# VectorE's mixing-table work in another order: differences in the second unit of four, carry scans in the last

## The chip, the cores and the metric

The kernel runs on one core of a Trainium2 chip. The metric is the device time of one execution in microseconds; the time before is 500.8 us, the median of three runs.

## The reference

Input x is 2 x 2048 tokens of 256 channels, float32. Cut to what matters:

```python
xn = layernorm(x)
# token mixing
k, v = xn @ key_w.T, xn @ value_w.T            # k is not used
r = sigmoid(xn @ recep_w.T)
aa, bb, pp = 0, 0, -10000
for t in range(T):                              # per batch row and channel
    ww = time_first + pp;  p = max(pp, ww)
    e1, e2 = exp(pp - p), exp(ww - p)
    wkv[t] = (e1*aa + e2*v[t]) / (e1*bb + e2 + 1e-6)
    ww2 = time_decay + pp; p2 = max(pp, ww2)
    e1b, e2b = exp(pp - p2), exp(ww2 - p2)
    aa = e1b*aa + e2b*v[t];  bb = e1b*bb + e2b;  pp = p2
attn = (r * wkv) @ out_w.T
# feed-forward: 8 experts, 2 for each token, and a shared one
gate = softmax(xn @ gate_w.T + gate_b); top 2 of 8
y = sum over the chosen e of gate_e * ((silu(xn@w1_e.T+b1_e) * (xn@w3_e.T+b3_e)) @ w2_e.T + b2_e)
z = (silu(xn@ws1.T+bs1) * (xn@ws3.T+bs3)) @ ws2.T + bs2
out = x + attn + y + z
```

The exponent pp, the decays e1b, the factors e1 and e2 and the sum bb depend on the time step and the channel only, not on x. So they can be computed once for all batch rows: 3 tables of 256 channels x 2048 steps. These are the mixing tables.

## The kernel before, in words

The program has three stages, written by hand for each engine, with semaphores between the engines and nothing that reorders: an engine runs its instructions in the order of the code.

1. `route`: the layer norm, the gate and the sorting of the tokens by expert.
2. `run_experts`: 71 tiles of 128 tokens go through their experts' weights, in 36 **units** `a` (`DUOS`): the first has one tile, the others two. Each product is made of three fp32r matmuls of high and low parts.
3. `mix`: eight steps of the token mixing, the shared expert and the sum.

The change lies in `run_experts`. What each engine does in unit `a` there:

- TensorE: turns the hidden rows (`turn_h(a)`, L1105, tile `ps_h`), turns the gathered tokens of unit a+3 (`turn_x`, L1079, `ps_x`), the down product of unit a-1 and the up product of unit a+2 (L1085, `ps_y` and `ps_g`). `turn_h(a)` waits for `hid` of unit a and for `h_lo` of unit a-1.
- ScalarE: silu of unit a+1 (L1161, `act`), the high parts of `ps_h` and `ps_x` (L1168, L1153), the result of unit a-1 (L1174), and pieces of the table work.
- VectorE: `hidden(a+1)` (L1249, tile `hid`, waits for that silu), `cut_h(a)` (L1256, `h_lo`), `cut_x(a+3)` (L1240, `x_lo`), and then its share of the table work.
- GpSimd: the indirect DMAs that gather the tokens of unit a+6 (L1008, `xg`), and its share of the table work. The gather of unit b waits until `turn_x(b-4)` is done (four buffers).
- SyncE: stores and loads.

The mixing tables are made beside this, in 8 **pieces** v of 256 time steps, four units for each. With v, r = divmod(a, 4), the work of piece v goes through these steps:

- `grown(v)`, VectorE: a copy of the last column to the first (L1264, `s_p`), then two scans (L1266) that give the exponent pp along the piece.
- `differences(v)`, VectorE: four scalar_tensor_tensor of 128x256 (L1277), (s_p + first) - s_p and (s_p + decay) - s_p, into `dif`, which lies in the tile `raw_vr` and has one buffer. It waits for `t_sides`, ScalarE's reading of the piece before.
- `halves(v)` and `exps(v)`, ScalarE: the positive and negative parts (L1182 to L1184, then `t_sides`) in unit 4v, and the exponentials (L1189 to L1194, with two loads of activation tables) in unit 4v+1. Piece 0 has both in unit 2.
- `scan_b(v)`, VectorE: a copy and two scans (L1286, L1289, `s_b`) in unit 4v+2; piece 0 has the scans alone in unit 3.
- `denominator(v)`, GpSimd: L1019, L1020 and L1022, tile `den`, in unit 4v+3 after the gather; it waits for `t_bb` (scan_b).
- `invert(v, 0..3)`, VectorE: four reciprocals of 128x128 (L1298), two in unit 4v+4, and one each in the next two.
- `factors(v)`, GpSimd: a product of 128x1024 (L1027) in unit 4v+6, once `t_rec` says that the fourth reciprocal is done.

In unit 24 GpSimd also makes the low parts of a table of biases (`low_rows`, L1033, L1034, L1037).

Before, `grown(v+1)` stood in unit 4v+1, ahead of the third reciprocal of piece v-1, and `differences(v+1)` in unit 4v+3. So VectorE's table work of a piece is: two reciprocals in r = 0; a copy, two scans and a reciprocal in r = 1; a copy, two scans and a reciprocal in r = 2; four differences in r = 3.

Of the kernel before, what the change touches and what calls it, by code (L numbers as in the profile page):

```python
# [85 lines left out]
def at_least(eng, sem, value):  # L86

    if isinstance(value, int) and value <= 0:
        return
    eng.wait_ge(sem, value)  # L90
# [766 lines left out]
def run_experts(nc, kept, placed, xn_d, y_d, y, y_stored, firsts1, coef_stored, tab_d, vec_tf, vec_td, ident, tile_tok, tile_exp,  # L857
# [3 lines left out]
    with ExitStack() as ctx:  # L861
# [6 lines left out]
        def sem(name):  # L868
            return kept.enter_context(nc.semaphore(name))
# [64 lines left out]
        t_dif = sem("t_dif")  # L934
# [18 lines left out]
        LAST_V = NPIECE - 1  # L953
# [279 lines left out]
        def vector(dve):  # L1233
            def cut_x(a):
                if a >= DUOS:
                    return
                n = tiles(a)
                dve.wait_ge(c_xhi, a + 1)
                at_least(dve, c_g, a - 1)
                nc.vector.tensor_tensor(x_lo[a % 2][:, 0:n], ps_x[:, 0:n], x_hi[a % 2][:, 0:n].bitcast(F32),  # L1240
                                        ALU.subtract).then_inc(c_xlo, 1)

            def hidden(a):
                if a >= DUOS:
                    return
                n = tiles(a)
                dve.wait_ge(c_silu, a + 1)
                at_least(dve, c_th, a)
                nc.vector.tensor_tensor(hid[:, 0:n, :], ps_g[a % 2][:, 0:n, FF:2 * FF], act1[:, 0:n, :],  # L1249
                                        ALU.mult).then_inc(c_h, 1)  # L1250

            def cut_h(a):
                n = tiles(a)
                dve.wait_ge(c_hhi, a + 1)
                at_least(dve, c_y, a - 1)
                nc.vector.tensor_tensor(h_lo[a % 2][:, 0:n], ps_h[:, 0:n], h_hi[a % 2][:, 0:n].bitcast(F32),  # L1256
                                               ALU.subtract).then_inc(c_hlo, 1)

            def grown(v):
                own = OwnIn(dve, t_own, At(0, v, NPIECE), 2)  # L1260
                if v == 0:
                    own.n += 1
                else:
                    own.link(nc.vector.tensor_copy(s_p[:, :, 0:1], s_p[:, :, PIECE:PIECE + 1]))  # L1264
                for c in range(KC):
                    ins = nc.vector.tensor_tensor_scan(out=s_p[:, c, 1:PIECE + 1],  # L1266
                                                       data0=grow[:, c:c + 1].broadcast_to([P, PIECE]),
                                                       data1=zero[:].broadcast_to([P, PIECE]),
                                                       initial=s_p[:, c, 0:1], op0=ALU.add, op1=ALU.add)
                own.link(ins)  # L1270
                own.close()

            def differences(v):
                at_least(dve, t_sides, v)
                for n, vec in enumerate((vec_tf, vec_td)):
                    for c in range(KC):
                        ins = nc.vector.scalar_tensor_tensor(out=dif[:, n, c, :], in0=s_p[:, c, 0:PIECE],  # L1277
                                                             scalar=vec[:, c:c + 1], in1=s_p[:, c, 0:PIECE],
                                                             op0=ALU.add, op1=ALU.subtract)
                ins.then_inc(t_dif, 1)  # L1280

            def scan_b(v):
                dve.wait_ge(t_exp, v + 1)
                if v > 0:
                    dve.wait_ge(t_den, v)
                    nc.vector.tensor_copy(s_b[:, :, 0:1], s_b[:, :, PIECE:PIECE + 1]).then_inc(t_carry, 1)  # L1286
                    dve.wait_ge(t_carry, v + 1)
                for c in range(KC):
                    ins = nc.vector.tensor_tensor_scan(out=s_b[:, c, 1:PIECE + 1], data0=decay[:, c, :],  # L1289
                                                       data1=one[:].broadcast_to([P, PIECE]), initial=s_b[:, c, 0:1],  # L1290
                                                       op0=ALU.mult, op1=ALU.add)
                ins.then_inc(t_bb, 1)

            def invert(v, i):
                c, h = divmod(i, 2)
                part = den[:, c, h * (PIECE // 2):(h + 1) * (PIECE // 2)]
                dve.wait_ge(t_den, v + 1)
                ins = nc.vector.reciprocal(part, part)  # L1298
                if i == 2 * KC - 1:
                    ins.then_inc(t_rec, 1)  # L1300

            def low_mask():
                own = Own(dve, c_mask)
                dve.wait_ge(c_iota, 1)
                own.link(nc.vector.tensor_scalar(row32[:], row32[:], TERMS - 1, None, ALU.bitwise_and))
                nc.vector.tensor_scalar(is_lo[:, 0:1], row32[:], float(3 * E + 1), None, ALU.is_equal)
                own.link(nc.vector.tensor_scalar(is_lo[:, 1:2], row32[:], float(2 * E), None, ALU.is_ge))
                own.link(nc.vector.tensor_tensor(is_lo[:, 1:2], is_lo[:, 1:2], is_lo[:, 0:1], ALU.subtract))
                own.mark(nc.vector.tensor_scalar(is_lo[:, 2:3], is_lo[:, 1:2], -2.0, 1.0, ALU.mult, ALU.add))
# [24 lines left out]
            for a in range(DUOS):  # L1334
                v, r = divmod(a, 4)
                hidden(a + 1)
                if a == DUOS - 1:
                    dve.wait_ge(c_whi, 2)
                    nc.vector.tensor_tensor(col[2][:], col[0][:], col[1][:].bitcast(F32), ALU.subtract
                                            ).then_inc(c_wlo, 1)  # L1340
                cut_h(a)
                cut_x(a + 3)
                if a < 2:
                    for i in range(12 + 2 * a, 14 + 2 * a):
                        split_lo(dve, i)
                if a == 1:
                    grown(0)
                    differences(0)
                if a == 2:
                    dve.wait_ge(t_dif, 1)  # L1350
                    grown(1)
                if a == 3:
                    scan_b(0)
                if r == 0 and 0 < v <= NPIECE:
                    invert(v - 1, 0)
                    invert(v - 1, 1)
                if r == 1:
                    if 0 < v < LAST_V:
                        grown(v + 1)
                    if 0 < v <= NPIECE:  # L1360
                        invert(v - 1, 2)
                    if v == NPIECE:
                        invert(v - 1, 3)
                if r == 2:
                    if 0 < v < NPIECE:
                        scan_b(v)
                    if 0 < v < NPIECE:
                        invert(v - 1, 3)
                if r == 3 and v < LAST_V:
                    differences(v + 1)  # L1370
                if a == A_ZERO + 2:
                    low_mask()

        return sync, gpsimd, tensor, scalar, vector, (c_y, c_yc, c_wlo, c_gT, c_rowsb)


# [483 lines left out]
```

## Time and profile before

| | |
|---|---|
| median of the runs | 500.8 us |
| the three runs | 498.76, 500.80, 504.41 us |
| span of the profiled execution, first to last instruction | 476.0 us |
| TensorE busy | 442.4 us (93%) |
| VectorE busy | 370.7 us (78%) |
| ScalarE busy | 241.5 us (51%) |
| GpSimd busy | 235.9 us (50%) |
| granted TensorE clock, mean over the span | 0.982 |

The profiled execution has its span on record and no time of its own beside it; 500.8 less 476.0 leaves 24.8 us that lie around the span. Times in the rows count from the span's start. The units of `run_experts` fill the time from about 74 to 267 us. In a row of the timeline the first number is the start, the second the time until the end of the last of the merged instructions, "x2" their count, and the bracket the idle time of the engine before it and what ended it. An instruction of VectorE can begin some hundredths of a us before the one ahead has ended, so starts are compared with starts where it matters.

### The profile page before, as it was taken

The numbers are of one execution on the slowest core, as the hardware profiler recorded it, in microseconds if no ns is written. First come the engines' busy times: TensorE is split into PE (matmuls) and PEld (weight loads), VectorE is DVE, ScalarE is ACT, GpSimd is POOL, SyncE is SP. The second block draws the span as 40 slices with busy tenths as digits, with TensorE's granted clock in tenths as the row PEclk, the third lists the DMA queues.
The fourth block names the chain that finished last, engine by engine and source line by source line (L and its number), as shares of the span: only waits on it lengthen the run. The fifth ranks groups of instructions, "written<-read, shape, count | busy, mean of one in ns | idle before, by whom it ended". The sixth has DMA issues, their size and how long they took to land.

```text
span 476.0 us, 8336 instructions
## 1 busy us (share of the span) xinstructions
PE 442.4 (93%) x2532; PEld 370.7 (78%) x2532; DVE 370.7 (78%) x700; ACT 241.5 (51%) x396; POOL 235.9 (50%) x222
## 2 busy tenths in 40 slices
PE   0886987988999999999999899999999999999997
PEld 0652464877888888888888778898898989898987
DVE  6967896968788898788776589996868687877863
ACT  4684845488586685958565633332414132423131
POOL 5041787726648685679845286752342516070000
PEclk9999959999999999999999999999999999999999
DMA  6899953335764665343473793735353444432001
GB/s 182 281 349 330 277 88 91 105 140 180 270 232 160 216 209 185 115 152 101 145 189 122 250 323 90 228 104 152 125 148 123 121 150 132 154 108 72 23 23 44
DMA packets 45858, 77.24 MB, mean 162 GB/s; under 512 B 5908, under 2 KB 32252, under 8 KB 45820
## 3 DMA queue, kind: packets, MB, share of 16 engines
q1 hardware_dynamic: 37580, 55.87, 34.0%
q0 software_dynamic: 8240, 20.88, 16.9%
q8 instruction: 21, 0.34, 0.3%
q14 instruction: 17, 0.14, 0.1%
HBM read 48.52 MB, written 28.21 MB: 161 GB/s over the span
## 4 chain that ended last, share of the span: by engine, by line
PE 46%; POOL 17%; DVE 14%; issue 13%; ACT 4%; DMA 4%; SPq 0%; POOLq 0%; DVEq 0%; ACTq 0%
POOL xg L1008 8%; PE ps_w L1545 5%; PE ps_w L1547 5%; PE ps_w L1546 5%; PE ps_w L1611 5%; PE ps_w L1610 5%; PE ps_w L1612 5%; PE ps_g L1085 4%; DMA w_lo<-w_all 2%; POOL den L1020 2%; PE ps_y L1085 2%; POOL den L1019 2%; DVE stats L678 2%; POOL col L1027 2%; POOL firsts L1027 2%
## 5 line engine op out<-in xcount | busy, mean ns | idle before, releaser
L1008 POOL DMA_INDIRECT xg<-xn_rows,tile_tok x71 | 72.7, 1024 | 20.7 <-issue 18.5
L1521 POOL DMA_INDIRECT yg<-expert_rows,rows x64 | 67.8, 1060 | 23.6 <-issue 17.1
L1085 PE MATMUL ps_g<-w_hi,x_hi 128*128 x142 | 56.2, 396 | 1.9 <-DVE x_lo L1240 1.9
L1085 PE MATMUL ps_g<-w_lo,x_hi 128*128 x142 | 56.3, 396 | 0.0
L1085 PE MATMUL ps_g<-w_hi,x_lo 128*128 x142 | 56.1, 395 | 0.0
L1652 ACT ACTIVATE sact<-ps_w,vec_b 128x512 f32<-128x512 f32 x32 | 22.0, 687 | 58.2 <-PE ps_w L1547 58.2
L1545 PE MATMUL ps_w<-col_hi,s_hi 128*128 128x512 f32 x128 | 50.5, 395 | 0.4 <-DVE shid L1763 0.4
L1546 PE MATMUL ps_w<-col_lo,s_hi 128*128 128x512 f32 x128 | 50.2, 392 | 0.0
L1547 PE MATMUL ps_w<-col_hi,s_lo 128*128 128x512 f32 x128 | 50.2, 392 | 0.0
L1085 PE MATMUL ps_y<-w_hi,h_hi 128*128 x142 | 43.1, 304 | 1.3 <-DVE h_lo L1256 1.3
L1249 DVE TENSOR_TENSOR hid<-ps_g,act 128x512 f32<-128x512 f32 (+1 forms) x36 | 23.7, 657 | 24.6 <-ACT act L1161 24.6
L1161 ACT ACTIVATE act<-ps_g 128x512 f32<-128x512 f32 (+1 forms) x36 | 21.3, 591 | 37.6 <-PE ps_g L1085 37.5
L1085 PE MATMUL ps_y<-w_hi,h_lo 128*128 x142 | 40.0, 282 | 0.0
L1085 PE MATMUL ps_y<-w_lo,h_hi 128*128 x142 | 39.9, 281 | 0.0
L1516 POOL COPY rows<-slots 128x8 int32<-128x8 int32 (+1 forms) x8 | 6.3, 785 | 65.4 <-DVE res L1733 56.6
L1763 DVE SCALAR_TENSOR_TENSOR shid<-ps_w,vec_b,sact 128x512 f32<-128x512 f32 x32 | 24.0, 750 | 17.1 <-ACT sact L1652 16.7
L1298 DVE RECIPROCAL den<-den 128x128 f32<-128x128 f32 x32 | 29.0, 929 | 10.5 <-POOL den L1022 10.2
L1611 PE MATMUL ps_w<-s_lo,s_hi 128*128 128x256 f32 x128 | 35.9, 280 | 0.0
L1612 PE MATMUL ps_w<-s_hi,s_lo 128*128 128x256 f32 x128 | 35.9, 280 | 0.0
L1610 PE MATMUL ps_w<-s_hi 128*128 128x256 f32 x128 | 35.9, 280 | 0.0
L1646 ACT ACTIVATE a_hi<-rw 128x1024 fp32r<-128x1024 f32 x8 | 8.5, 1059 | 48.0 <-PE ps_w L1612 43.2
L1085 PEld LDWEIGHTS ps_g<-w_hi,x_hi 128*128 128x128 f32 x142 | 26.7, 188 | 7.3 <-issue 2.4
(247 smaller groups left out, 1286.3 us busy)
## 6 DMA issues: line engine op xcount, KB each, us to landing
expert_rows<-y SPq DMA_DIRECT2D x35, 256.0 KB, 2.3
w_lo<-w_all SPq DMA_DIRECT2D x16, 384.0 KB, 10.3
table<-mix_tables SPq DMA_DIRECT2D x8, 768.0 KB, 5.8
xin<-x SPq DMA_DIRECT2D x16, 256.0 KB, 3.5
xn_rows<-xn SPq DMA_DIRECT2D x16, 256.0 KB, 5.2
xn_columns<-xT SPq DMA_DIRECT2D x8, 512.0 KB
col<-xn_columns SPq DMA_DIRECT2D x8, 512.0 KB, 4.7
res<-x SPq DMA_DIRECT2D x16, 256.0 KB, 2.9
```

The costliest lines, as they stand in the source:

```text
L1008: pool.indirect_dma_start(out=xg[b][:, t, :], out_offset=None, in_=xn_d[:, :], in_offset=bass.IndirectOffsetOnAxis(ap=tile_tok[:, first_ti ...
L1085: mm = nc.tensor.matmul(out, x[:, k, :], w[:, ds(e, 1), k, cols].rearrange("p o n -> p (o n)"), start=(k == 0 and n == 0), stop=(last and ...
L1249: nc.vector.tensor_tensor(hid[:, 0:n, :], ps_g[a % 2][:, 0:n, FF:2 * FF], act1[:, 0:n, :], ALU.mult).then_inc(c_h, 1)
L1298: ins = nc.vector.reciprocal(part, part)
L1521: pool.indirect_dma_start(out=yg[a.buf(2)][:, k, q, :], out_offset=None, in_=y_d[:, :], in_offset=bass.IndirectOffsetOnAxis(ap=picked[a.bu ...
L1545: nc.tensor.matmul(out, w_hi, x_hi, start=start, stop=False)
L1546: nc.tensor.matmul(out, w_hi, x_lo, start=False, stop=False)
L1547: return nc.tensor.matmul(out, w_lo, x_hi, start=False, stop=stop)
L1610: nc.tensor.matmul(out, hi[:, k, cols], w_hi[:, k, :], start=start, stop=False)
L1611: nc.tensor.matmul(out, hi[:, k, cols], w_lo[:, k, :], start=False, stop=False)
L1612: return nc.tensor.matmul(out, lo[:, k, cols], w_hi[:, k, :], start=False, stop=stop)
L1763: nc.vector.scalar_tensor_tensor(out=hid[m % 2][:], in0=ps_w[m % 2 * 2 + 1][:], scalar=vec_b3[:, m:m + 1], in1=act1[m % 2][:], op0=ALU.add ...
```

## The change

`differences(v+1)` goes from unit 4v+3 to unit 4v+1, and `grown(v+2)` takes its place in unit 4v+3, so the exponent of a piece is now scanned five units before ScalarE reads its differences, instead of three. At the start, `differences(1)` is put ahead of `scan_b(0)` in unit 3, and `grown(2)` behind it. The wait on `t_dif` ahead of `grown` asks for differences that the same engine issued earlier. No instruction is added or taken away, and nothing moves on another engine.

```diff
                     dve.wait_ge(t_dif, 1)
                     grown(1)
                 if a == 3:
+                    differences(1)
                     scan_b(0)
...
                 if r == 1:
                     if 0 < v < LAST_V:
-                        grown(v + 1)
+                        differences(v + 1)
                     if 0 < v <= NPIECE:
                         invert(v - 1, 2)
...
                     if 0 < v < NPIECE:
                         invert(v - 1, 3)
-                if r == 3 and v < LAST_V:
-                    differences(v + 1)
+                if r == 3 and v + 2 <= LAST_V:
+                    dve.wait_ge(t_dif, v + 2)
+                    grown(v + 2)
```

The first place is VectorE in unit 3 and at the start of unit 4. `s_b` and `s_p` are the sums and exponents, `raw_vr` holds the differences; the order prints a scan as SCALAR_TENSOR_TENSOR too, the scans are L1266 and L1289. Before:

```order
L1240 TENSOR_TENSOR x_lo<-ps_x,x_hi 128x512
L1289 SCALAR_TENSOR_TENSOR s_b<-decay_t,s_b,one 128x256 x2
L1277 SCALAR_TENSOR_TENSOR raw_vr<-s_p,vec_tf 128x256 x2
L1277 SCALAR_TENSOR_TENSOR raw_vr<-s_p,vec_td 128x256 x2
L1249 TENSOR_TENSOR hid<-ps_g,act 128x512
```

And now, the same place:

```order
L1240 TENSOR_TENSOR x_lo<-ps_x,x_hi 128x512
L1277 SCALAR_TENSOR_TENSOR raw_vr<-s_p,vec_tf 128x256 x2
L1277 SCALAR_TENSOR_TENSOR raw_vr<-s_p,vec_td 128x256 x2
L1289 SCALAR_TENSOR_TENSOR s_b<-decay_t,s_b,one 128x256 x2
L1264 COPY s_p<-s_p 128x2
L1266 SCALAR_TENSOR_TENSOR s_p<-grow,s_p,zero 128x256 x2
L1249 TENSOR_TENSOR hid<-ps_g,act 128x512
```

The four differences now stand ahead of the scans of `s_b`, and a copy and two scans of `s_p` have come in behind them, ahead of `hid` of unit 5.

The second place is VectorE in units 5 to 7 (r = 1, 2, 3 of piece 1), from the `x_lo` of unit 5 to the `hid` in unit 8. Before:

```order
L1240 TENSOR_TENSOR x_lo<-ps_x,x_hi 128x512
L1264 COPY s_p<-s_p 128x2
L1266 SCALAR_TENSOR_TENSOR s_p<-grow,s_p,zero 128x256 x2
L1298 RECIPROCAL den<-den 128x128
...
L1286 COPY s_b<-s_b 128x2
L1289 SCALAR_TENSOR_TENSOR s_b<-decay_t,s_b,one 128x256 x2
L1298 RECIPROCAL den<-den 128x128
...
L1277 SCALAR_TENSOR_TENSOR raw_vr<-s_p,vec_tf 128x256 x2
L1277 SCALAR_TENSOR_TENSOR raw_vr<-s_p,vec_td 128x256 x2
L1249 TENSOR_TENSOR hid<-ps_g,act 128x512
```

And now:

```order
L1240 TENSOR_TENSOR x_lo<-ps_x,x_hi 128x512
L1277 SCALAR_TENSOR_TENSOR raw_vr<-s_p,vec_tf 128x256 x2
L1277 SCALAR_TENSOR_TENSOR raw_vr<-s_p,vec_td 128x256 x2
L1298 RECIPROCAL den<-den 128x128
...
L1286 COPY s_b<-s_b 128x2
L1289 SCALAR_TENSOR_TENSOR s_b<-decay_t,s_b,one 128x256 x2
L1298 RECIPROCAL den<-den 128x128
...
L1264 COPY s_p<-s_p 128x2
L1266 SCALAR_TENSOR_TENSOR s_p<-grow,s_p,zero 128x256 x2
L1249 TENSOR_TENSOR hid<-ps_g,act 128x512
```

The differences and the copy with its scans have changed places; the unit between them is as it was. Pieces 2 to 5 read alike, and in piece 6 (unit 27) nothing of either stands in the last unit now.

## Rows read from the trace of the kernel before

**Rows 1.** The head of the page: the span, and TensorE's busy time.
```profile
span 476.0 us, 8336 instructions
...
PE 442.4 (93%) x2532; PEld 370.7 (78%) x2532; DVE 370.7 (78%) x700; ACT 241.5 (51%) x396; POOL 235.9 (50%) x222
```

**Rows 2.** Busy time of each engine in one stretch (us, then the count of instructions).
```profile
111.00:209.00 98.00, 98.00 (x617) 86.74 (x617) 81.08 (x133) 70.83 (x122) 63.77 (x59) 1.00 0.59 195
```

**Rows 3.** Timeline of TensorE, turn_h of units 5, 11 and 30.
```profile
110.44 0.63 PE L1105 MATMUL ps_h<-ident,hid 128*128 128x128 f32 x4 [1.53 <-DVE h_lo L1256]
...
141.28 0.60 PE L1105 MATMUL ps_h<-ident,hid 128*128 128x128 f32 x4
...
239.12 0.63 PE L1105 MATMUL ps_h<-ident,hid 128*128 128x128 f32 x4 [0.59 <-DVE h_lo L1256]
```

**Rows 4.** Timeline of VectorE, table work of units 1 to 3.
```profile
92.88 0.88 DVE L1277 SCALAR_TENSOR_TENSOR raw_vr<-s_p,vec_tf 128x256 f32<-128x256 f32 x2
...
96.27 0.15 DVE L1264 COPY s_p<-s_p 128x2 f32<-128x2 f32 x1
96.46 1.39 DVE L1266 TENSOR_TENSOR_SCAN s_p<-grow,s_p,zero 128x256 f32<-128x256 f32 x2
...
103.81 1.39 DVE L1289 TENSOR_TENSOR_SCAN s_b<-decay_t,s_b,one 128x256 f32<-128x256 f32 x2
105.11 1.81 DVE L1277 SCALAR_TENSOR_TENSOR raw_vr<-s_p,vec_tf 128x256 f32<-128x256 f32 x2
106.83 2.26 DVE L1277 SCALAR_TENSOR_TENSOR raw_vr<-s_p,vec_td 128x256 f32<-128x256 f32 x2
109.02 0.68 DVE L1249 TENSOR_TENSOR hid<-ps_g,act 128x512 f32<-128x512 f32 x1
```

**Rows 5.** Timeline of GpSimd, denominator of piece 0, and the same product of piece 2.
```profile
105.28 1.35 POOL L1019 TENSOR_TENSOR den<-col,s_b 128x512 f32<-128x512 f32 x1 [8.57 <-DVE s_b L1289]
106.71 1.35 POOL L1020 TENSOR_TENSOR den<-den,col 128x512 f32<-128x512 f32 x1
108.15 0.67 POOL L1022 TENSOR_SCALAR den<-den 128x512 f32<-128x512 f32 x1
...
147.68 1.20 POOL L1019 TENSOR_TENSOR den<-col,s_b 128x512 f32<-128x512 f32 x1
```

**Rows 6.** Timeline of VectorE in units 9 to 11 (r = 1 to 3 of piece 2).
```profile
133.85 0.33 DVE L1264 COPY s_p<-s_p 128x2 f32<-128x2 f32 x1
...
138.53 0.69 DVE L1249 TENSOR_TENSOR hid<-ps_g,act 128x512 f32<-128x512 f32 x1 [1.92 <-ACT act L1161]
139.13 0.68 DVE L1256 TENSOR_TENSOR h_lo<-ps_h,h_hi 128x512 fp32r<-128x512 f32 x1
...
144.41 1.53 DVE L1277 SCALAR_TENSOR_TENSOR raw_vr<-s_p,vec_tf 128x256 f32<-128x256 f32 x2
```

**Rows 7.** Timeline of GpSimd beside the rows of VectorE just shown.
```profile
134.50 1.23 POOL L1008 DMA_INDIRECT xg<-xn_rows,tile_tok  x1 [0.30 <-issue]
...
137.28 0.95 POOL L1008 DMA_INDIRECT xg<-xn_rows,tile_tok  x1 [0.30 <-issue]
142.84 2.42 POOL L1027 TENSOR_TENSOR firsts<-firsts,den 128x1024 f32<-128x1024 f32 x1 [4.62 <-DVE den L1298]
145.41 0.99 POOL L1008 DMA_INDIRECT xg<-xn_rows,tile_tok  x1
```

**Rows 8.** Timeline of GpSimd's low rows.
```profile
214.82 2.88 POOL L1033 TENSOR_SCALAR rows<-rows,is_lo 128x1024 f32<-128x1024 f32 x1
217.66 2.85 POOL L1034 TENSOR_SCALAR rows_hi<-rows_hi,is_lo 128x1024 fp32r<-128x1024 f32 x1
220.60 2.40 POOL L1037 TENSOR_TENSOR rows_b<-rows,rows_hi 128x1024 fp32r<-128x1024 f32 x1
```

**Rows 9.** Timeline of VectorE in unit 25, beside the first of them.
```profile
215.70 0.27 DVE L1264 COPY s_p<-s_p 128x2 f32<-128x2 f32 x1
```

**Rows 10.** Timeline of VectorE in unit 28, the reciprocals of piece 6.
```profile
236.07 1.76 DVE L1298 RECIPROCAL den<-den 128x128 f32<-128x128 f32 x2 [2.85 <-POOL den L1022]
```

## The prediction, made before the changed kernel was run

> **What bounds the kernel now.** The head of the page comes first: a span of 476.0 us, of which TensorE is busy for 442.4 [rows 1]. Then the stretches of the experts' stage, where the change lies: from 111 to 209 us TensorE is busy for 98.00 of 98.00 us, while VectorE has 81 and GpSimd 64 [rows 2]. So for most of that stage nothing that VectorE does between two of its deadlines can be seen in the time; only a stop of TensorE can. The third view is TensorE's timeline, read for the brackets. From turn_h(5) to turn_h(11) six units take 30.84 us, 5.1 us each. Between unit 5 and the end of the piece work there are two stops: 1.53 us ahead of turn_h(5) at 110.44, and 0.59 us ahead of turn_h(30) at 239.12 [rows 3]. A reader should see that both end with VectorE's h_lo, which stands right behind hid. So the question is what holds VectorE up ahead of hid there, and for that the timelines of VectorE and GpSimd are laid side by side.
>
> At 110.44: VectorE ran scan_b(0) from 103.81, the four differences of piece 1 from 105.11, and hid of unit 5 only at 109.02 [rows 4]. Its input was there long before (no bracket on the row). The two vec_tf differences of piece 0 took 0.88 us [rows 4]; the four here took 109.02 - 105.11 = 3.91, because GpSimd's denominator of piece 0 ran beside them: L1019 to 106.63, L1020 to 108.06, L1022 to 108.82 [rows 5]. The pairs end at 106.92 and 109.09, each some 0.3 us after an instruction of GpSimd: one difference gets in for each of them.
>
> At 239.12 it is GpSimd: low rows, gathers, factors and denominator stand one behind the other there, and the reciprocals ahead of hid sat idle for 2.85 us, to 236.07, until the denominator came [rows 10].
>
> **The change part by part.** The instructions are the same, 16 scans and 32 differences among them. What is moved is where they meet others.
>
> 1. Unit 3, the differences first. GpSimd waits for scan_b(0) (8.57 us idle [rows 5]), so nothing runs against them. Two cost 0.88 with their overlap, 0.80 from start to start; four cost 1.6, from 103.81 to 105.4. Then scan_b(0), 1.39 us, to T = 106.8.
>
> 2. Unit 3, grown(2) behind it. The copy (0.15) and the scans (0.19 from the copy's start, then 1.39 [rows 4]) are new ahead of hid of unit 5. And now they run beside the denominator: it started 0.09 us after scan_b's end before (103.81 + 1.39 = 105.20, and 105.28 [rows 4, 5]), so it starts at 106.9, and the first scan wants to start at 106.9 too. No row shows scans of s_p beside a product of GpSimd, so I bound it:
>  - no collision: scans end by 108.3, hid at 108.3, which is 0.7 earlier than 109.02;
>  - the first scan gets in, then L1019 (1.20 us alone [rows 5]), then the second scan: 106.9 + 0.7 + 1.2 + 0.7 = 109.5, 0.4 later;
>  - L1019 gets in first: 106.9 + 1.2 + 0.7 (scan) + 1.3 (L1020) + 0.7 = 110.8, 1.7 later.
>  The nearest rows are the differences beside the same instructions, where VectorE's ran first and GpSimd got in after it (L1019 took 1.35 there, 1.20 alone [rows 5]). I take the middle: +0.4 us. The stop of 1.53 becomes about 1.9.
>
> The Trainium skill bears on this ("SBUF — State Buffer", section "Who interferes with whom"): a VectorE instruction with two inputs in SBUF contends with a GpSimd one that reads SBUF, and whoever issues first has the shared ports for its whole instruction while the other waits in full. This trace agrees for the differences: the four beside the denominator took 3.91 us. A scan reads two inputs too, and so by that rule the first case above, -0.7, falls away. Without the rule all three stay open, as I keep them.
>
> 3. Unit 3, everybody else. GpSimd's denominator is 1.6 us later and its gathers with it. Behind the gathers of a piece GpSimd sits idle until the reciprocals are done (4.62 us in piece 1's factors [rows 7]), so this is hidden. ScalarE's halves(1) had waited for the differences; they now come 3.7 us earlier, but TensorE doesn't wait for silu there: nothing.
>
> 4. r = 1 of pieces 1 to 6, differences for copy and scans. Before, copy, scans and reciprocal went from 133.85 to about 136.6; then VectorE sat idle for 1.92 us until silu, and h_lo ended at 139.81, 1.3 us before turn_h(11) at 141.28 could have noticed, with 0.15 for the signal [rows 3, 6]. So this unit has 1.9 + 1.3 = 3.2 us to spare. The differences alone take 1.6 against 1.8 for copy and scans. What runs beside them is gathers. Beside the gather at 145.41 (0.99 us [rows 7]) they went through at full speed: the pair of vec_tf, of which the first had to wait for L1027's end at 145.26, was over at 145.94, 0.68 us later [rows 6, 7]. Cost: nothing, between -0.2 and the rival below.
>
> 5. r = 3 of pieces 1 to 5, copy and scans for differences. Before, the first difference started at 144.41 and stood behind L1027 (142.84 to 145.26 [rows 7]); with 0.8 for the other pair the four were over at 146.7. Now the copy stands behind L1027 instead, until 145.3, and the scans end at 146.7. The same end, and TensorE had no stop behind it before [rows 2]. But the scans now run beside the gather at 145.41. The gather that ran beside scans at 134.50 took 1.23 us, the one at 137.28 0.95 [rows 7]: +0.25 us for GpSimd. This matters only where GpSimd is late, at turn_h(30): +0.25 us, if all of it arrives.
>
> 6. Unit 25, differences(7) beside the low rows. The copy of before started at 215.70 within L1033 (214.82 to 217.70) and was over in 0.27 us [rows 8, 9]. That instruction of GpSimd didn't hold VectorE up, and I take nothing; the other end is a rival.
>
> 7. Unit 27 has neither any more. VectorE then waits for the denominator all the same [rows 10]: nothing. The wait on t_dif is for the engine's own earlier work: nothing. Queues of SyncE and GpSimd keep their order, and the reload of raw_vr waits for halves(7), which stays in unit 28. The mix stage starts earlier or later by what the stage before gives.
>
> Sum against the profiled execution: 476.0 + 0.4 + 0.25 = 476.7 us of span. The 24.8 us around it stay, so against the median of 500.8 it is 501.5 us.
>
> **The rivals.**
>
> - A, the forecast: one collision in unit 3, 501.5 us.
> - B, GpSimd's product first: +1.7 + 0.25, about 502.8 us. The gap of 0.02 us between the two starts speaks for it; against it, a waiting VectorE instruction that is dispatched a hair earlier wins, as the first difference did.
> - C, no collision of scans: -0.7 + 0.25 at most, 500.3 us. For it speaks that the scans of unit 25, right behind that copy, ran beside L1033 as fast as elsewhere; against it, the gather of 1.23 us beside scans.
> - D, the slower side: in r = 1 each of the four differences gets in only between two gathers. Before, the gathers of this unit ended at 138.23 [rows 7]. With three further differences pushed between them (0.4 each) that is 139.4, then the last difference and the reciprocal (0.4 + 0.95): hid at 140.8 instead of 138.53, 2.3 us later, of which 1.3 are to spare. That is 0.9 us for each of six pieces, 5.6 in all, and with the forecast's 0.7 it gives 507.1 us. It decides only from the point where the work of r = 1 is longer than 2.75 + 3.2 = 6.0 us. Against it: the differences beside the gather at 145.41. For it: the copy at 133.85 took 0.33 instead of 0.15 beside a gather, and ended with it.
> - E, the low rows hold differences(7): one gets in behind L1033 (217.70), one behind L1034 (220.51), the rest behind L1037 (223.00) [rows 8]. With the reciprocal VectorE is free at 224.4 instead of 220.3: 4.1 later, less 1.3 to spare, and some 0.3 of it comes back at turn_h(30): +2.5 on top of A, 504.0 us. Against it stands the copy at 215.70 [rows 9], which no instruction of GpSimd held up to its end.
>
> The same section of the Trainium skill has it that a two-input instruction takes only the read side, and that writing descriptors needs the write side (marked there as inferred). By that D couldn't be, and the time would be that of A, B or C. The differences beside the gather at 145.41 agree; the longer gather beside scans doesn't fit well.
>
> **How the numbers follow.** A 0.38, B 0.25, C 0.20, D 0.05, E 0.08, and 0.04 for what I don't see. A, B and C lie within 500.3 and 502.8, all within 0.5% of before; E is 0.6% above. A measurement of this kernel can tell about 1% from no change (its three runs lie from 498.8 to 504.4). So within 1%: 0.91 for A, B, C and E, less 0.01 for a shift of the measurement: 0.90. Slower by over 1%: D and a part of E with B, 0.06. Faster by over 1% (below 495.8): no term reaches it, 0.04 for the unseen and the measurement. The range takes A, B, C and E and the scatter of a median of such runs, about 1.3 us below C: 499.0 to 504.2 us.
>
> **What would show it.** In the changed profile: the four differences of piece 1 start at 103.8 and take 1.6 us; the copy and scans of grown(2) stand beside L1019, and their length tells A (2.7 us from copy to hid), B (4.0) and C (1.6) apart; turn_h(5) starts at 110.8 with a bracket of 1.9 (A), 3.3 (B) or 0.8 (C). The rows of L1277 have a mean near 0.47 us for both kinds in place of 0.91 and 0.56; the copies of L1264 become longer, near 0.9 us each. From 111 to 209 us TensorE stays without a stop. The stop at turn_h(30) is 0.6 to 0.9 us. I would be wrong if a bracket on turn_h appears in r = 2 or r = 3 units (D), if one appears at turn_h(27) (E), or if the span moves by over 3 us.

## The result, and the profile after

The changed kernel takes 505.1 us (median of 22 runs, 501.7 to 508.9) against 502.6 us for the kernel before in the same measurement (22 runs, 498.1 to 504.9). The ratio is 1.005, with an interval of 1.003 to 1.007. So it is slower by a little, some 2.4 us: less than 1%, on the side where the forecast of 501.5 us pointed (+0.7 us), but over three times as much, and outside its range of 499.0 to 504.2 us. (Here and below a median takes all runs, while a ratio leaves out runs that lie over 1.5% above the fastest of the same kernel.)

The head of the page of the changed kernel, and the busy time of its engines:

```profile
span 503.7 us, 8331 instructions
...
PE 457.1 (91%) x2532; PEld 379.4 (75%) x2532; DVE 368.5 (73%) x700; ACT 242.2 (48%) x396; POOL 234.1 (46%) x222
```

Against [rows 1] the span is 27.7 us longer, and that isn't the change. The runs of the changed kernel come with their spans, and a run takes 1.8 us more than its span (505.5 with 503.7). By that the execution of [rows 1], with its 476.0 us, would be a run of 478 us, which is 20 us below the fastest of the 22 runs of before, and 11 us below its fastest run in any set (489.0 us). It was another kind of execution (on which chip isn't on record; before has medians of 493.9, 496.8 and 498.3 us on the three chips of the experiments, still 16 us or more above), and my 24.8 us "around the span" don't exist. Experiment e1 shows a common one.

What the change did has to be read at its own place then. VectorE in unit 3 and at the start of unit 4, which answers to [rows 4]:

```profile
110.00 0.87 DVE L1277 SCALAR_TENSOR_TENSOR raw_vr<-s_p,vec_tf 128x256 f32<-128x256 f32 x2
110.79 0.88 DVE L1277 SCALAR_TENSOR_TENSOR raw_vr<-s_p,vec_td 128x256 f32<-128x256 f32 x2
111.58 1.39 DVE L1289 TENSOR_TENSOR_SCAN s_b<-decay_t,s_b,one 128x256 f32<-128x256 f32 x2
112.89 0.14 DVE L1264 COPY s_p<-s_p 128x2 f32<-128x2 f32 x1
113.07 3.38 DVE L1266 TENSOR_TENSOR_SCAN s_p<-grow,s_p,zero 128x256 f32<-128x256 f32 x2
116.48 0.69 DVE L1249 TENSOR_TENSOR hid<-ps_g,act 128x512 f32<-128x512 f32 x1
```

The same two scans of s_p apart, in a narrower look at that timeline:

```profile
113.07 1.73 DVE L1266 TENSOR_TENSOR_SCAN s_p<-grow,s_p,zero 128x256 f32<-128x256 f32 x1
...
114.72 1.73 DVE L1266 TENSOR_TENSOR_SCAN s_p<-grow,s_p,zero 128x256 f32<-128x256 f32 x1
```

GpSimd beside them, which answers to [rows 5]:

```profile
113.06 1.19 POOL L1019 TENSOR_TENSOR den<-col,s_b 128x512 f32<-128x512 f32 x1 [11.49 <-DVE s_b L1289]
114.33 1.57 POOL L1020 TENSOR_TENSOR den<-den,col 128x512 f32<-128x512 f32 x1
115.99 0.87 POOL L1022 TENSOR_SCALAR den<-den 128x512 f32<-128x512 f32 x1
```

And turn_h of units 4 and 5 on TensorE, which answers to the first row of [rows 3]:

```profile
109.64 0.63 PE L1105 MATMUL ps_h<-ident,hid 128*128 128x128 f32 x4 [2.00 <-DVE h_lo L1256]
117.92 0.63 PE L1105 MATMUL ps_h<-ident,hid 128*128 128x128 f32 x4 [1.28 <-DVE h_lo L1256]
```

The four differences take 1.6 us now, from 110.00 to 111.58, where they took 3.9 [rows 4]. But the two scans of s_p take 3.38 us instead of 1.39: L1019 of GpSimd started at 113.06, the first scan at 113.07, and it was over 1.73 us later, behind the end of L1019 (114.25); the second took 1.73 us too and was over at 116.45, behind L1020 (115.90). From the first instruction of the table work in unit 3 to hid it is 116.48 - 110.00 = 6.48 us, where it was 109.02 - 103.81 = 5.21 [rows 4]. From turn_h(4) to turn_h(5) it is 117.92 - 109.64 = 8.28 us.

The bracket at turn_h(5), 1.28 us, is shorter than the 1.53 of before [rows 3], although the unit is longer. The reason is TensorE's own clock. In this stretch, and in the same one of e11 below, a second execution of the changed kernel (stretch, its length, busy time of TensorE, its weight loads, VectorE, ScalarE and GpSimd, then the granted clock, the DMA share and GB/s):

```profile
109.64:117.92 8.28, 7.00 (x33) 5.96 (x33) 8.21 (x13) 4.38 (x8) 4.42 (x4) 0.79 0.50 190
...
104.09:112.33 8.24, 5.47 (x32) 4.42 (x33) 8.17 (x13) 4.51 (x8) 4.38 (x4) 1.00 0.50 191
```

Here the granted clock was 0.50 from 111 to 113 us, the level of 1.2 GHz, after TensorE had sat idle for 2.00 us ahead of turn_h(4); its work took 7.00 us and left it less to wait. In e11 the clock stayed at 1.00 (2.4 GHz), the work took 5.47 us, and the bracket is 2.78. VectorE is busy almost throughout both, and the stretch has the same length. So it is the distance between two turn_h that shows what VectorE costs, and not the bracket.

VectorE's groups by line show the same as totals (busy us, mean ns of one):

```profile
L1266 DVE TENSOR_TENSOR_SCAN s_p<-grow,s_p,zero 128x256 f32<-128x256 f32 x16 | 13.4, 879 | 0.2
...
L1277 DVE SCALAR_TENSOR_TENSOR raw_vr<-s_p,vec_tf 128x256 f32<-128x256 f32 x16 | 7.1, 483 | 0.0
```

The reader sees a trap here. Almost all of the 32 differences are at full speed now (the other half, vec_td, has a mean of 480 ns), and VectorE is busy for 368.5 us instead of 370.7, 2.2 us less. The program is slower all the same, because of two scans in one unit that TensorE waits for.

### The profile page after: what moved, and what is told of

The parts are those of the page before. It is cut to its first block, busy times and chain, and to the rows that moved or that the text cites. A ratio compares the mean times of both kernels' runs of the same rounds, so it can differ in the third digit from the quotient of the medians.

```text
span 503.7 us, 8331 instructions
## 1 busy us (share of the span) xinstructions
PE 457.1 (91%) x2532; PEld 379.4 (75%) x2532; DVE 368.5 (73%) x700; ACT 242.2 (48%) x396; POOL 234.1 (46%) x222
## 4 chain that ended last, share of the span: by engine, by line
PE 46%; POOL 19%; issue 16%; DVE 10%; DMA 3%; SPq 3%; ACT 2%; POOLq 0%; DVEq 0%; ACTq 0%
POOL xg L1008 8%; PE ps_w L1549 5%; PE ps_w L1547 5%; PE ps_w L1548 5%; PE ps_w L1613 5%; PE ps_w L1612 5%; PE ps_w L1614 5%; PE ps_g L1085 4%; POOL w_lo L381 3%; DMA w_lo<-w_all 2%; POOL den L1020 2%; DVE stats L678 2%; PE ps_y L1085 2%; POOL den L1019 2%; SPq L426 2%
## 5 line engine op out<-in xcount | busy, mean ns | idle before, releaser
L1008 POOL DMA_INDIRECT xg<-xn_rows,tile_tok x71 | 70.1, 988 | 26.6 <-issue 17.9
L1523 POOL DMA_INDIRECT yg<-expert_rows,rows x64 | 64.9, 1014 | 23.6 <-issue 17.9
L1085 PE MATMUL ps_g<-w_hi,x_hi 128*128 x142 | 57.5, 405 | 3.3 <-issue 3.3
L1549 PE MATMUL ps_w<-col_hi,s_lo 128*128 128x512 f32 x128 | 51.5, 402 | 1.4 <-issue 1.4
L1547 PE MATMUL ps_w<-col_hi,s_hi 128*128 128x512 f32 x128 | 51.9, 405 | 0.2 <-issue 0.2
L1548 PE MATMUL ps_w<-col_lo,s_hi 128*128 128x512 f32 x128 | 51.4, 402 | 0.0
L1518 POOL COPY rows<-slots 128x8 int32<-128x8 int32 (+1 forms) x8 | 8.1, 1010 | 73.3 <-DVE res L1735 64.5
L1747 DVE TENSOR_TENSOR res<-ps_w,res 128x256 f32<-128x256 f32 x32 | 12.8, 421 | 37.3 <-PE ps_w L1614 21.5
```

The source lines that it names most:

```text
L1008: pool.indirect_dma_start(out=xg[b][:, t, :], out_offset=None, in_=xn_d[:, :], in_offset=bass.IndirectOffsetOnAxis(ap=tile_tok[:, first_ti ...
L1085: mm = nc.tensor.matmul(out, x[:, k, :], w[:, ds(e, 1), k, cols].rearrange("p o n -> p (o n)"), start=(k == 0 and n == 0), stop=(last and ...
L1523: pool.indirect_dma_start(out=yg[a.buf(2)][:, k, q, :], out_offset=None, in_=y_d[:, :], in_offset=bass.IndirectOffsetOnAxis(ap=picked[a.bu ...
L1547: nc.tensor.matmul(out, w_hi, x_hi, start=start, stop=False)
L1548: nc.tensor.matmul(out, w_hi, x_lo, start=False, stop=False)
L1549: return nc.tensor.matmul(out, w_lo, x_hi, start=False, stop=stop)
```

## The experiments

Three sets ran on three chips, each set on one chip together with the kernel before. Theory T is: the cost is the collision of the scans of s_p with the denominator's products in unit 3, and nothing else of the change matters. Each kernel's times come with one profiled execution; what the profiles are read for is the time from turn_h(4) to turn_h(5) on TensorE, which in e1 is 7.00 us.

### e1: the kernel before, once more

No edit.

> The kernel before, unchanged, for a second profile: its first one has a span of 476.0 us, while the changed kernel's runs take 1.7 us more than their spans (505.5 against 503.7), so a run of before of 502.6 us should have a span near 501. Theory T (unit 3's collision and nothing else is new): ratio 1.000, span near 501 us, a stop of 1.5 us ahead of turn_h(5), and the same kind of idle time in the mix stage marked 'issue' as in the changed kernel (PE and its weight loads some 10 to 15 us), which the first profile of before doesn't have. Rival R (the change itself causes these stops in the later stages): span near 476, no such stops.

Measured: 495.9 us against 496.8 us, ratio 0.998 (0.995 to 1.001). The head of the page, and turn_h of units 4, 5, 10, 11, 24 and 30:

```profile
span 496.7 us, 8336 instructions
```

```profile
106.54 0.63 PE L1105 MATMUL ps_h<-ident,hid 128*128 128x128 f32 x4 [2.07 <-DVE h_lo L1256]
113.54 0.63 PE L1105 MATMUL ps_h<-ident,hid 128*128 128x128 f32 x4 [1.54 <-DVE hid L1249]
...
139.28 0.60 PE L1105 MATMUL ps_h<-ident,hid 128*128 128x128 f32 x4
145.27 0.63 PE L1105 MATMUL ps_h<-ident,hid 128*128 128x128 f32 x4
...
214.61 0.60 PE L1105 MATMUL ps_h<-ident,hid 128*128 128x128 f32 x4
...
247.17 0.63 PE L1105 MATMUL ps_h<-ident,hid 128*128 128x128 f32 x4 [0.89 <-DVE hid L1249]
```

The span is 496.7 us in a run of 498.5. In unit 3 nothing differs from the first profile of before: 7.00 us between the turn_h, the stop of 1.5. But elsewhere there is idle time that the first profile didn't have. From turn_h(10) to turn_h(11) it takes 5.99 us instead of 5.1, with no wait for another engine in the bracket. And the waits of this execution have rows that were absent there, such as this one (total us, times, longest):

```profile
DVE res L1745 <- remote: 15.4, 4, 5.7
```

They stand in the changed kernel's profile too (DVE res 15.8 us in 5 waits). So these stops belong to a common execution of either kernel, and rival R for the late stages is out. What started them isn't in these rows, and I don't name a cause. But they aren't the whole difference. The last stage in the first profile of before and in e1:

```profile
262.00:476.00 214.00, 208.66 (x1210) 182.48 (x1208) 163.91 (x253) 68.53 (x94) 76.53 (x80) 1.00 0.41 132
...
270.00:496.70 226.70, 215.16 (x1211) 185.60 (x1209) 163.24 (x253) 68.71 (x95) 75.17 (x80) 0.98 0.38 125
```

Of the 12.7 us that e1 takes longer here, TensorE is busy for 6.5 with the same matmuls. After it had worked for only 2.2 of the 5 us from 305 to 310 in e1, its granted clock was 0.53 from 310 to 321 us. Such a stretch of half clock stands in the last stage of each of the other profiles too, twelve in all; only the first one of before has none there.

### e3 and e4: the start alone, the later pieces alone

e3, against the kernel before:

```diff
                 if a == 3:
+                    differences(1)
                     scan_b(0)
+                    dve.wait_ge(t_dif, 2)
+                    grown(2)
...
-                    if 0 < v < LAST_V:
+                    if 1 < v < LAST_V:
                         grown(v + 1)
...
-                if r == 3 and v < LAST_V:
+                if r == 3 and 0 < v < LAST_V:
                     differences(v + 1)
```

> Only the start of the change: unit 3 as in the changed kernel (differences(1), scan_b(0), grown(2)), pieces from 2 on as before (grown in r = 1, differences in r = 3). Theory T: the whole cost is here, scans of 3.4 us beside L1019 and L1020 in unit 3, a ratio to before of 1.003 to 1.005. Rival R: ratio 1.000.

e4, against the changed kernel:

```diff
                 if a == 3:
-                    differences(1)
                     scan_b(0)
+                    differences(1)
...
                     invert(v - 1, 1)
+                if a == 4:
+                    dve.wait_ge(t_dif, 2)
+                    grown(2)
...
-                if r == 3 and v + 2 <= LAST_V:
+                if r == 3 and 0 < v <= LAST_V - 2:
```

> Only the later pieces of the change: unit 3 as before (scan_b(0), differences(1)), grown(2) in unit 4 behind the two reciprocals, and from unit 5 on as in the changed kernel. Theory T: unit 3 takes 5.2 us from x_lo to hid as before, the stop at turn_h(5) is 1.5 us, ratio 1.000 to 1.001. Rival R: ratio 1.004 to 1.005, with new stops ahead of turn_h in r = 2 or 3.

Measured: e3 498.4 us, ratio 1.0047 (1.0015 to 1.0079), e4 496.2 us, ratio 0.9989 (0.9966 to 1.0012). The start alone has the cost of the whole change, the later pieces alone have none. In e3 VectorE and TensorE:

```profile
108.31 3.36 DVE L1266 TENSOR_TENSOR_SCAN s_p<-grow,s_p,zero 128x256 f32<-128x256 f32 x2
111.70 0.69 DVE L1249 TENSOR_TENSOR hid<-ps_g,act 128x512 f32<-128x512 f32 x1
```

```profile
104.87 0.63 PE L1105 MATMUL ps_h<-ident,hid 128*128 128x128 f32 x4 [2.07 <-DVE h_lo L1256]
113.14 0.63 PE L1105 MATMUL ps_h<-ident,hid 128*128 128x128 f32 x4 [1.28 <-DVE h_lo L1256]
```

Scans of 3.36 us and 8.27 us between the turn_h, as in the changed kernel. In e4, the differences of unit 3 again beside the denominator, 7.00 us between the turn_h, and the later stretch from turn_h(24) to turn_h(30):

```profile
106.38 0.63 PE L1105 MATMUL ps_h<-ident,hid 128*128 128x128 f32 x4 [2.07 <-DVE h_lo L1256]
113.38 0.63 PE L1105 MATMUL ps_h<-ident,hid 128*128 128x128 f32 x4 [1.54 <-DVE hid L1249]
...
213.67 0.60 PE L1105 MATMUL ps_h<-ident,hid 128*128 128x128 f32 x4
...
246.26 0.63 PE L1105 MATMUL ps_h<-ident,hid 128*128 128x128 f32 x4 [1.37 <-DVE h_lo L1256]
```

The last two rows answer to those of e1. The stop ahead of turn_h(30) is 1.37 us in e4 and 0.89 in e1, which looks like a cost of 0.5 us. But from turn_h(24) to turn_h(30) it is 246.26 - 213.67 = 32.59 us in e4 and 247.17 - 214.61 = 32.56 in e1. The end of that stretch is set by GpSimd's row of work (from L1027 at 212.18 to the end of L1022 at 244.09 it is 31.91 us in e1, and 31.93 in e4); where TensorE lost less on the way, it waits longer at the end. The profiles of the changed kernel and of the other experiments agree: 32.55 to 32.61 us in eight of ten, in either order of the later pieces, and 33.07 and 33.08 in e5 and e6.

### e2 and e6: the collision taken away in two ways

e2, against the changed kernel, moves grown(2) ahead of scan_b(0), so that GpSimd is released after the scans of s_p:

```diff
                 if a == 3:
                     differences(1)
+                    dve.wait_ge(t_dif, 2)
+                    grown(2)
                     scan_b(0)
...
-                if r == 3 and v + 2 <= LAST_V:
+                if r == 3 and 0 < v <= LAST_V - 2:
```

> The changed kernel with one more move: grown(2) stands ahead of scan_b(0) in unit 3, not behind it. Theory T (the scans of s_p wait for the denominator's products in unit 3: 3.38 us instead of 1.39): the scans take 1.39 again, from x_lo to hid 4.55 us instead of 6.48 (before 5.21), the stop at turn_h(5) falls to about 0.9 us; time 2.0 us below the changed kernel, ratio to before 0.998 to 1.001. Rival R (the later pieces cost the time): ratio stays at 1.004 to 1.005. Rival S (the denominator's start, now 1.6 us later, costs it): the ratio rises above 1.005.

Measured: 496.2 us, ratio 0.9988 (0.9956 to 1.0020). VectorE in unit 3:

```profile
108.92 0.87 DVE L1277 SCALAR_TENSOR_TENSOR raw_vr<-s_p,vec_tf 128x256 f32<-128x256 f32 x2
...
110.82 1.40 DVE L1266 TENSOR_TENSOR_SCAN s_p<-grow,s_p,zero 128x256 f32<-128x256 f32 x2
...
113.56 0.67 DVE L1249 TENSOR_TENSOR hid<-ps_g,act 128x512 f32<-128x512 f32 x1
```

The same instructions as in the changed kernel's unit 3, and 4.64 us where that took 6.48; the scans of s_p are back at 1.40 us. TensorE has 6.42 us between the turn_h.

e6 leaves VectorE's order as changed and makes GpSimd wait instead. It is the cleanest test, since on VectorE nothing differs:

```diff
                 pool.wait_ge(t_bb, v + 1)
+                if v == 0:
+                    pool.wait_ge(t_own, 6)
```

> The changed kernel with VectorE's order untouched; GpSimd's denominator of piece 0 waits until grown(2) is done as well, so nothing of GpSimd runs beside the scans. Theory T: the two scans take 1.39 us instead of 3.4, 6.4 us from turn_h(4) to turn_h(5) instead of 8.3, ratio 1.9 us (0.004) below e5. Rival V (the scans are slow there for a reason of their own, their data or the copy ahead of them): the scans stay at 3.4 us and the ratio at e5's. Rival S (a later denominator costs at the reciprocals): the scans are short, but a new stop of 1 us or more stands ahead of turn_h(6).

It ran beside e5, the changed kernel unchanged:

> The changed kernel, unchanged, beside the three that follow and on their chip. Theory T (the scans of s_p in unit 3 collide with the denominator's products; 1.3 us from turn_h(4) to turn_h(5): 8.27 against 7.00): ratio to before 1.002 to 1.006, 8.3 us between the two turn_h. Theory U (there is no difference beyond chance and the first measurement was one side of it): ratio 0.998 to 1.001.

Measured: e5 493.9 us, ratio 1.001 (0.998 to 1.004); e6 490.9 us, ratio 0.993 (0.990 to 0.996). e6 is 3.0 us below e5, where T said 1.9. VectorE, GpSimd and TensorE in e6 (its lines lie two further on: L1268 is the scan of s_p, L1021 the first product of the denominator, L1107 turn_h):

```profile
108.84 0.87 DVE L1279 SCALAR_TENSOR_TENSOR raw_vr<-s_p,vec_tf 128x256 f32<-128x256 f32 x2
...
111.90 1.39 DVE L1268 TENSOR_TENSOR_SCAN s_p<-grow,s_p,zero 128x256 f32<-128x256 f32 x2
113.33 0.69 DVE L1251 TENSOR_TENSOR hid<-ps_g,act 128x512 f32<-128x512 f32 x1
```

```profile
113.44 1.19 POOL L1021 TENSOR_TENSOR den<-col,s_b 128x512 f32<-128x512 f32 x1 [12.91 <-DVE s_p L1268]
```

```profile
108.47 0.63 PE L1107 MATMUL ps_h<-ident,hid 128*128 128x128 f32 x4 [1.58 <-DVE h_lo L1258]
114.76 0.63 PE L1107 MATMUL ps_h<-ident,hid 128*128 128x128 f32 x4 [0.82 <-DVE h_lo L1258]
120.07 0.60 PE L1107 MATMUL ps_h<-ident,hid 128*128 128x128 f32 x4
```

The scans take 1.39 us; 6.29 us between turn_h(4) and turn_h(5), and no stop at turn_h(6). So rival V (slow for a reason of their own) and rival S (a later denominator costs) are out. Against before, e5 is 1.3 us and e6 2.3 us below what T gives; the third set asks whether that comes again.

### e7 and e8: the start without the scans

e7 is the kernel before with only the differences of unit 3 put first:

```diff
                 if a == 3:
+                    differences(1)
                     scan_b(0)
...
-                if r == 3 and v < LAST_V:
+                if r == 3 and 0 < v < LAST_V:
                     differences(v + 1)
```

> The kernel before with one edit: in unit 3 the four differences stand ahead of scan_b(0), and nothing comes in behind it. By T the differences take 1.6 us instead of 3.9 since GpSimd's products start only behind them, unit 3 takes 3.0 us from x_lo to hid instead of 5.2, the stop ahead of turn_h(5) is gone: 5.3 us between the two turn_h instead of 7.0, and the ratio to before is 0.996 to 0.998 (1.7 us less). If the later denominator (1.6 us) takes it back, the stop appears at turn_h(6) and the ratio is 0.999 to 1.001.

e8 is the changed kernel with grown(2) in unit 4, behind the reciprocals:

```diff
                     invert(v - 1, 1)
+                if a == 4:
+                    dve.wait_ge(t_dif, 2)
+                    grown(2)
...
-                if r == 3 and v + 2 <= LAST_V:
+                if r == 3 and 0 < v <= LAST_V - 2:
```

> The changed kernel with grown(2) taken from unit 3 to unit 4, behind the two reciprocals; the later pieces in the changed order. T: no stop at turn_h(5); in unit 4 the copy and the scans (1.6 us) come behind reciprocals that wait for a later denominator, so a stop of about 0.8 us at turn_h(6): 0.9 us less than before, ratio 0.997 to 0.999. If the later pieces' order costs anything of its own, it stands 0.002 above e7 or more.

Measured: e8 492.0 us against 493.9, ratio 0.997 (0.994 to 1.000). e7 493.0 us, 0.85 us less than before; the ratio given for it, 0.990 (0.984 to 0.995), rests on five of its twelve runs, those up to 490.7 us; the others lie from 492.8 to 496.1. So it isn't used. In the profiles, unit 3 of e7:

```profile
102.93 0.87 DVE L1277 SCALAR_TENSOR_TENSOR raw_vr<-s_p,vec_tf 128x256 f32<-128x256 f32 x2
...
105.82 0.67 DVE L1249 TENSOR_TENSOR hid<-ps_g,act 128x512 f32<-128x512 f32 x1
```

```profile
102.56 0.63 PE L1105 MATMUL ps_h<-ident,hid 128*128 128x128 f32 x4 [2.78 <-DVE h_lo L1256]
107.86 0.60 PE L1105 MATMUL ps_h<-ident,hid 128*128 128x128 f32 x4
112.98 0.60 PE L1105 MATMUL ps_h<-ident,hid 128*128 128x128 f32 x4
```

2.89 us instead of 5.21, and 5.30 us between the turn_h: the stop of before is gone and doesn't come back at turn_h(6). In e8 it comes back in part:

```profile
104.64 0.63 PE L1105 MATMUL ps_h<-ident,hid 128*128 128x128 f32 x4 [1.77 <-DVE h_lo L1256]
109.94 0.60 PE L1105 MATMUL ps_h<-ident,hid 128*128 128x128 f32 x4
116.06 0.63 PE L1105 MATMUL ps_h<-ident,hid 128*128 128x128 f32 x4 [0.85 <-DVE h_lo L1256]
```

### e9, e10, e11: a third chip

The kernels of e7, e6 and e5 once more.

> e7 once more, since its twelve runs fell into two groups, around 488 and around 494 us. By T it takes 1.7 us less than before (5.3 us from turn_h(4) to turn_h(5), 7.0 before): ratio 0.995 to 0.999. If e7's lower group was the kernel's own, the ratio is 0.990 again.

> e6 once more: by T 0.6 us less than before (6.4 us from turn_h(4) to turn_h(5)), ratio 0.997 to 1.000. If the 0.993 of the first time was more than chance, it comes again, and something beside unit 3 has to give 2.5 us.

> The changed kernel beside them. T: 8.27 us from turn_h(4) to turn_h(5), ratio to before 1.001 to 1.005, and 1.9 us above e10, 3.0 above e9.

Measured: before 498.3 us; e9 497.2 us, ratio 1.000 (0.996 to 1.004); e10 497.7 us, 0.999 (0.996 to 1.003); e11 500.1 us, 1.004 (1.000 to 1.008). By the medians e11 stands 2.4 us above e10 (T: 1.9) and 3.0 above e9 (T: 3.0). The 0.993 of e6 and the 0.990 of e7 didn't come again. The profile of e9 has 6.71 us between the two turn_h, without a wait in the bracket, and that of e11 8.24; e10 has 6.29 again. The e9 stretch isn't VectorE's: hid stands 2.88 us behind the first difference, as in e7. It is the granted clock. From turn_h(4) to turn_h(5) in e9, and from turn_h(5) to turn_h(6) in e11:

```profile
105.62:112.33 6.71, 6.71 (x33) 6.11 (x34) 5.11 (x10) 3.79 (x7) 3.11 (x3) 0.75 0.48 180
...
112.33:119.15 6.82, 6.82 (x32) 5.99 (x33) 6.30 (x11) 6.03 (x9) 5.20 (x6) 0.75 0.36 102
```

TensorE is busy all through both, at 0.75 on average. In e9 the clock was 0.50 from 106 to 109 us, after an idle time of 2.07 us ahead of turn_h(4); in e11 it was 0.50 from 114 to 116, after one of 2.78 ahead of turn_h(5). At full clock such a unit takes 5.30 us, so that is 1.4 and 1.5 us. It doesn't follow each such stop: in e7 and e10 the clock stayed at 1.00 after 2.78 and 2.66 us.

All together (us from turn_h(4) to turn_h(5) in the profile; the same to turn_h(7), less the 17.41 us of e1; median against the kernel before on the same chip):

| kernel | turn_h(4) to (5) | turn_h(4) to (7), less 17.41 | time against before |
|---|---|---|---|
| changed (first measurement; e5; e11) | 8.28; 8.27; 8.24 | +1.3; +1.3; +2.8 | +2.4; 0.0; +1.8 |
| e3, start alone | 8.27 | +1.3 | +1.7 |
| e1, before; e4, later alone | 7.00; 7.00 | 0; 0 | -0.8; -0.6 |
| e2, scans ahead | 6.42 | -0.6 | -0.6 |
| e6, e10, GpSimd waits | 6.29; 6.29 | -0.7; -0.7 | -3.0; -0.6 |
| e8, grown(2) in unit 4 | 5.30 | -0.7 | -1.9 |
| e7, e9, differences first | 5.30; 6.71 | -1.9; +0.4 | -0.9; -1.2 |

The first two rows have a mean of +1.5 in the last column, the others a mean of -1.2, and single values scatter by 1 to 2 us: e1, the same kernel, shows -0.8.

## Why the prediction was wrong, and where it was right

**The side and the mechanism** were right: the forecast had the scans of unit 3 collide with the denominator, and that is shown by e3 (the start alone, ratio 1.0047), e4 (all but the start, 0.9989) and e6 (only GpSimd's start moved; scans 1.39 instead of 3.4 us).

**Step 2 failed in its size.** It bounded the cost at -0.7, +0.4 and +1.7 us and took the middle, "the first scan gets in, then L1019". In all four profiles of that order the other case came: L1019 at 113.06, the scan at 113.07, and the same in e3 (108.30 and 108.31), e11 (107.51 and 107.52) and e5 (both at 107.64). I had computed a gap of 0.02 us in GpSimd's favour and then went by the differences of before, which were first because they started 0.17 us ahead of L1019, and no row showed who wins a tie. The term measured +1.27 us (6.48 less 5.21), 0.85 more than taken. It is less than case B's 1.7, since I had charged each scan 0.7 us behind the product it waits for, and 0.55 are left of it there (L1019's end at 114.25 to 114.80), of which L1020 loses 0.3.

**The base of the sum was off by more than any term.** "The 24.8 us around it stay": they were 1.8. The profile of before was an execution 20 us faster than any of the 22 runs, and the page's span against the runs' median was the sign, which I explained away. It did no harm to the difference, because unit 3 is the same in both profiles of before (7.00 us), and since the 24.8 us were the median less the span, they left the median as the base. But that was a median of three runs: by 22 runs before takes 502.6 us, not 500.8. Of the 3.6 us between forecast and result, 1.8 are this. Step 2 gives another 0.85, step 5 takes 0.25 back, and the 1.2 us that are left belong to no term of the sum.

**Step 1** was right: the differences take 1.6 us, and e7 shows what that alone is worth, a stop of 1.5 us gone on TensorE (in e9 the half clock covers it). **Step 3** was right: a denominator that starts 1.6 to 3.3 us later costs nothing (e6, e2, e7: no stop at turn_h(6)). **Step 4** was right, rival D didn't come. The differences of r = 1 beside the gathers, in the changed kernel:

```profile
143.17 0.88 DVE L1277 SCALAR_TENSOR_TENSOR raw_vr<-s_p,vec_td 128x256 f32<-128x256 f32 x2
```

0.88 us for the second pair, alongside a gather from 143.03 to 144.07. The copies of grown take longer, as the text expected: 0.87 us in the five r = 3 units.

**Step 5** was half right. The copy waits for L1027 as foreseen and the scans behind it end as the differences did, but the +0.25 us for GpSimd is nil: the gather beside them, at 155.40, took 0.97 us, not 1.2. VectorE in unit 11:

```profile
154.41 0.87 DVE L1264 COPY s_p<-s_p 128x2 f32<-128x2 f32 x1
155.31 1.45 DVE L1266 TENSOR_TENSOR_SCAN s_p<-grow,s_p,zero 128x256 f32<-128x256 f32 x2
```

What happened is the reverse: the copy ends at 155.28 with L1027 (152.84 to 155.25), and the scans took 1.45 instead of 1.39. And e4 against e1 shows the stretch up to turn_h(30) unchanged (32.59 and 32.56 us). The stop of 1.36 us that the changed kernel has there would have been read as a cost without it.

**Steps 6 and 7** were right: beside L1033 the differences of unit 25 took 0.93 and 0.87 us, and rival E didn't come. "From 111 to 209 us TensorE stays without a stop" was wrong by the profile (1.02 us at turn_h(11), 0.69 at turn_h(23)), and brackets in such units were to be the sign of rival D. But e3, where the later pieces are as before, has the same two (1.10 us at turn_h(11), 0.67 at turn_h(23)), and e1 a unit of 5.99 us at turn_h(11). So they aren't the change, and the sign was a poor one.

What stays open: T's 1.3 us is less than the 2.4 us of the first measurement (its interval is 1.4 to 3.6 us), and about the mean of the three, 1.4. One candidate for the rest was neither foreseen nor tested: the half clock after a longer stop, which cost e11 1.5 us in unit 5. (1 less the granted clock) times the span, as a mean over the runs, is 0.9, 0.2 and 1.7 us higher in e3, e5 and e11 than in before on the same chip, where a single mean is good to some 0.5; for the other eight experiments the same difference goes from -1.1 to +0.8. That points to it and doesn't show it. e7 is 1.9 us better than before in the profile and 0.9 and 1.2 us in the medians of e7 and e9; that it beats the kernel before isn't measured beyond chance. Against the changed kernel it is 0.9 us better in one set (493.0 against 493.9) and 3.0 in the other (497.2 against 500.1).

The Trainium skill's rule ("SBUF — State Buffer", section "Who interferes with whom") would have settled step 2 better than my nearest row did: whoever issues first gets the shared ports, the other waits. GpSimd's row starts 0.01 us earlier, and the scan ended only behind L1019. This trace agrees, and case C was out by that rule, as the text said. It differs in the length of the hold. The first scan ran on until 114.80, and if it had held the ports for its whole instruction, L1020, which started at 114.33, would have lost 0.47 us; it took 1.57 us against 1.28 alone (e2), so it lost 0.3.

## What to carry to other kernels

Before moving work of one engine, look at what its new neighbour releases: here the same move put the differences out of the way of GpSimd's products and the scans into it, and the cost that the profiles show for the collision is 1.3 us, in one unit of 36. A collision's price hangs on who starts first; where the two starts lie within some hundredths of a us, as here, no sum of rows decides it, and the dear case belongs in the forecast. And compare the span of the profiled execution with the runs' times before building a sum on it: a profile 20 us below the median is another execution than the one that gets measured. And look at the granted clock of a stretch before putting its length down to a wait: in e9 a unit lost 1.4 us with TensorE busy throughout.

## What the runs showed of the hardware that I had not expected

- A scan of 128x256 with two inputs in SBUF waits for a product of GpSimd that has begun (1.73 us instead of 0.73 for each of two), and delays the next product by 0.3 us, 1.57 against 1.28 us.
- A copy of two columns can wait for 2 us: in unit 26 of the changed kernel it ran from 232.83 to 234.92, and L1037 beside it from 232.50 to 234.90.
- GpSimd's tensor_scalar with one operation (L1033, 2.87 us for 1024 elements) lets VectorE's scans pass at full speed (1.39 us beside it in before), and its differences nearly so (0.93 us for the first two of unit 25); a copy took 0.27 us [rows 9] instead of 0.15. L1022, a tensor_scalar with two operations, held a difference of before until its end (the last of the four in [rows 4] ended at 109.09, L1022 at 108.82 [rows 5]).
- Executions of one program can differ by 20 us in span, 476.0 and 496.7 us for the kernel before: by idle times that no wait of the program explains, and by stretches of half clock behind them.
- After an idle time of 2.0 to 2.8 us TensorE's granted clock fell to 0.50 in some executions (e9, e11, the changed kernel's first) and stayed at 1.00 in others (e7, e10, e1).
